# Two post-norm decoder layers on one core: an order of work written out stage by stage and tile by tile, with a PSUM bank for every fill

## The reference

```
x = norm(x + latent attention(x))          # l0: 16 heads, 32 latents, rotary tables, causal softmax
x = norm(x + linear attention(ctx, x))     # x0: q (k^T v), its own norm with gain and offset
x = norm(x + fp4 gated ffn(x))             # f0: 704 wide; x, weights and hidden are quantized in blocks of 16
x = norm(x + attention(x))                 # l1: causal softmax, and a second product over e = v - y
x = norm(x + cross attention(x, ctx, mask))# x1: softmax, Wo, norm, a 1024 wide relu ffn, norm
x = norm(x + fp6 linear(x))                # f1: x and weight quantized in blocks of 32
```

## Time and profile before

| | |
|---|---|
| time, median of 3 runs | 926.42 us (926.02 to 926.56) |
| time of the profiled execution | 925.68 us |
| its span, first to last instruction | 923.9 us |
| mean granted TensorE clock | 0.978 |
| TensorE busy | 827.3 us, 90% |
| VectorE busy | 712.0 us, 77% |
| ScalarE busy | 637.5 us, 69% |
| GpSimd busy | 300.6 us, 33% |

### The profile page before, as it was taken

The page is one execution under the profiler, slowest core; times in us unless marked ns, Lnnn a source line. Parts: engine busy times, 40 slices in busy tenths (PEclk is TensorE's granted clock), DMA queues, the critical chain, the costliest instruction groups (busy, mean ns, idle before and its releaser), DMA issues.

```text
span 923.9 us, 29437 instructions
## 1 busy us (share of the span) xinstructions
PE 827.3 (90%) x11910; PEld 661.0 (72%) x11910; DVE 712.0 (77%) x1619; ACT 637.5 (69%) x2507; POOL 300.6 (33%) x554
## 2 busy tenths in 40 slices
PE   4576789999999999999999999999999999988873
PEld 3454567777878787878788787878787877867642
DVE  6886586878797878878787978788787878786552
ACT  2434669595968688786959686877869686856541
POOL 1121222233243434243333434342433334242221
PEclk8888999999999999999999999999999999999997
DMA  9300200000100000000001000000000000000000
GB/s 327 142 6 10 94 9 22 2 25 2 36 2 27 12 17 17 13 19 8 28 2 33 9 25 11 22 16 7 20 8 28 11 7 11 11 7 6 9 1 12
DMA packets 24440, 24.87 MB, mean 27 GB/s; under 512 B 2304, under 2 KB 22640, under 8 KB 24176
## 3 DMA queue, kind: packets, MB, share of 16 engines
q1 hardware_dynamic: 24304, 22.98, 7.6%
HBM read 18.80 MB, written 2.10 MB: 23 GB/s over the span
## 4 chain that ended last, share of the span: by engine, by line
PE 67%; ACT 18%; DVE 8%; POOL 3%; issue 2%; DMA 1%; SPq 0%; DVEq 0%; POOLq 0%; ACTq 0%
PE bank L1284 39%; PE s_tile L1284 21%; ACT prob L771 9%; PE bank L1405 3%; PE bank L1495 2%; ACT k_ L804 2%; POOL rstd L638 1%; DVE rope_ L1051 1%; ACT probT L710 1%; ACT x_ L819 1%; DVE stats L1001 1%; DVE y_ L1014 1%; ACT cross_ L795 1%; PE bank L1525 1%; ACT xt_ L856 1%
## 5 line engine op out<-in xcount | busy, mean ns | idle before, releaser
L771 ACT ACTIVATE prob<-s_tile,low 128x128 f32<-128x128 f32 x768 | 273.2, 402 | 6.6 <-DVE low L1059 6.5
L771 ACT ACTIVATION_READ_ACCUMULATOR prob<-s_tile,low 128x1 f32 x768 | 186.0, 242 | 0.0
L1059 DVE TENSOR_REDUCE low<-s_tile 128x4 f32<-128x512 f32 x192 | 121.1, 680 | 19.8 <-PE s_tile L1284 19.8
L636 POOL TENSOR_TENSOR var_eps<-mean_var,rsq 128x1 f32<-128x1 f32 x144 | 31.3, 218 | 267.3 <-DVE mean_var L1003 267.3
L710 ACT ACTIVATE probT<-bank 128x512 f32<-128x512 f32 x192 | 99.7, 618 | 24.0 <-PE bank L1495 23.9
L638 POOL TENSOR_TENSOR rstd<-var_eps,rsq 128x1 f32<-128x1 f32 x144 | 87.2, 606 | 11.3
L710 ACT ACTIVATE xt_<-bank 128x256 f32<-128x256 f32 x64 | 24.6, 384 | 87.5 <-PE bank L1405 87.3
L1284 PE MATMUL bank<-w_gu,xt_ 128*128 128x352 f32 x256 | 78.4, 459 | 0.6 <-ACT xt_ L710 0.6
L1495 PE MATMUL bank<-cst,prob 32*128 32x32 f32 x3072 | 61.6, 225 | 19.0 <-ACT prob L771 12.8
L1495 PEld LDWEIGHTS bank<-cst,prob 32*128 32x128 f32 x3072 | 54.0, 138 | 32.5 <-ACT prob L771 15.0
L673 POOL TENSOR_TENSOR k_<-q_,q_scale 128x256 f32<-128x256 f32 x32 | 19.8, 620 | 176.2 <-DVE q_ L962 176.2
(11 more groups left out here) (200 smaller groups left out, 1948.9 us busy)
## 6 DMA issues: line engine op xcount, KB each, us to landing
xtin<-in_xT SPq DMA_DIRECT2D x16, 128.0 KB, 2.3
next_<-in_x SPq DMA_DIRECT2D x16, 128.0 KB, 6.8
ct_<-in_ctxT SPq DMA_DIRECT2D x16, 128.0 KB, 7.5
w<-in_w SPq DMA_DIRECT2D x2, 1024.0 KB, 6.7
out<-x_ SPq DMA_DIRECT2D x16, 128.0 KB, 1.9
next_<-x_ SPq DMA_DIRECT2D x16, 127.0 KB
rowt<-in_rows SPq DMA_DIRECT2D x1, 1664.0 KB, 9.0
w<-in_gate_up SPq DMA_DIRECT2D x2, 512.0 KB, 6.5
```

The source lines that it names most:

```text
L636: pool.tensor_tensor(var_eps[:, b:b + 1], mean_var[:, b, 1:2], rsq[:, 0:1], ALU.add) .then_inc(eps_in, 1)
L771: ins = act.activation(prob[:, r, c * P:(c + 1) * P], bank[r][:, c * P:(c + 1) * P], ACT.Exp, bias=low[:, b, at0:at0 + 1], accum_out=sums[ ...
L1059: dve.tensor_reduce(low[:, b, 4 * r:4 * r + 4], rows4(src[:, :]), AX_X, ALU.max, negate=True)\
```

## The change

The two tables `START` and `SLOTS` go. In their place stands `ORDER_AT`, which gives each stage of each engine a place in that engine's order for every tile, so that the distance between tiles can differ from stage to stage and from tile to tile. `BANKS` gets a digit for each tile and fill. `COVERED` is written anew for the new order. Since the order no longer keeps certain distances by itself, four waits are added. The stages, their instructions and their number are the same on the four compute engines; on SP the entries that did nothing are no longer listed.

On TensorE the first places are now the seven stages warm0, 12, 1, 5, 7, 3 and 2, then l0_project of tile 0; all 14 warm stages stand in the first 49 places.

```diff
-START = (0, 2381, 4750, 7129, 9503, 11883, 14256, 16632, 19008, 21379, 23760, 26136, 28512, 30885, 33264,
-         35642)
-SLOTS = dict(
-    PE=dict(v_bias=0, turn_up0=1340, cproj_bias=4139, warm1=6077, l0_project=6248, x0_kv=8380, l0_lat=8504,
...
+ORDER_AT = dict(
+    PE=dict(warm0=0, warm12=1, warm1=2, warm5=3, warm7=4, warm3=5, warm2=6, l0_project=(7, 11, 19, 25, 32, 225, 243, 278,
+        311, 448, 467, 505, 536, 672, 693, 731), v_bias=8, l0_lat=(9, 14, 24, 28, 222, 241, 277, 309, 446, 465, 502,
...
+        x1_scores=(146, 178, 209, 246, 370, 400, 434, 470, 594, 623, 657, 695, 812, 846, 876, 893),
...
+    DVE=dict(quant_up0=0, columns=1, round_up0=2, v_bias=3, l0_rope=(4, 6, 17, 19, 171, 185, 216, 245, 351, 365, 396, 425,
...
-BANKS = {"p_g": 5, "p_qk0": 5, "p_qk1": 4, "p_v": 6, "l0_project.qk": 7, "l0_v.v": 5, "l0_lat.s0": 0,
...
+    "l0_mix0.t0": '5475633532073676', "l0_mix0.t1": '3551361767550005', "l0_mix0.t2": '4244027406144747',
...
-    steps = [(START[t] + slot[stage], t, n, stage) for n, stage in enumerate(STAGES) if stage in slot
-             for t in range(TILES)]
...
+    steps = [(n, stage, t) for stage, places in ORDER_AT[engine].items()
+             for t, n in enumerate(places if isinstance(places, tuple) else (places,))]
+    return [(stage, t) for _, stage, t in sorted(steps)]
...
                 pool.wait_ge(came_x[b], came_by(i, 1, 1))
+                if i > 0:
+                    wait_empty(pool, i - 1, ("f1_out", b, "o"))
                 pool.tensor_tensor(xb_[:, b, :], next_[:, b, :], cproj_bias, ALU.add).then_inc(x_biased, 1)
...
+                    if stage == "l0_out" and i > 0:
+                        normed(dve, i - 1, "f1_norm", b)
                     emptied(dve.tensor_tensor(y_[:, b, :], src[:, 0:D], other[:, b, :], ALU.add), i, key)
...
+                    if n == 2 and i + b > 0:
+                        dve.wait_ge(k_done, i * GROUP + b)
...
+                if i * GROUP + b >= 2:
+                    wait_full(dve, i, ("x1_scores", b - 2, "s3"))
```

More of the change, by code:

```diff
@@ L67 @@
 PIECES = ("up0", "up1", "up2", "down0", "down1", "last")
-START = (0, 2381, 4750, 7129, 9503, 11883, 14256, 16632, 19008, 21379, 23760, 26136, 28512, 30885, 33264,
-         35642)
-SLOTS = dict(
-    PE=dict(v_bias=0, turn_up0=1340, cproj_bias=4139, warm1=6077, l0_project=6248, x0_kv=8380, l0_lat=8504,
[L74 to L108, removed]
-)
@@ L190, in plan_banks @@
     used, where = [0] * 8, {}
-    fills = [(name, name) for name in SETUP_FILLS]
+    fills = [(name, BANKS[name]) for name in SETUP_FILLS]
     for stage, t in ORDER["PE"]:
-        fills += [(name, name) if stage in SETUP_STAGES else ((stage, t, name), stage + "." + name)
+        fills += [(name, BANKS[name]) if stage in SETUP_STAGES else ((stage, t, name), int(BANKS[stage + "." + name][t]))
                   for name in STAGE_FILLS.get(stage, [])]
-    for key, fill in fills:
-        k = BANKS[fill]
+    for key, k in fills:
         where[key] = (k, used[k])
@@ new lines @@
+    ("l0_mix0", "free.t3"): 0xf16a, ("l0_mix0", "l0_scores.s2"): 0xaddd, ("l0_mix1", "l0_scores.s3"): 0xbfff,
+    ("l0_mix2", "l0_scores.s0"): 0xfdd9, ("l0_mix3", "l0_scores.s1"): 0xccc9, ("l0_out", "free.o"): 0xad4e,
+    ("l0_out", "l0_value.y"): 0x2040, ("l0_project", "came_xT"): 0xeee0, ("l0_project", "free.qk"): 0xb9e8,
+    ("l0_scores", "free.s0"): 0x7cdb, ("l0_scores", "free.s1"): 0xffff, ("l0_scores", "free.s2"): 0xf7d5,
+    ("l0_scores", "free.s3"): 0xdd37, ("l0_scores", "k_done"): 0xaaaf, ("l0_scores", "l0_lat.s3"): 0x5550,
@@ new lines @@
+    ("l1_mix2", "l1_scores.s0"): 0x7fef, ("l1_mix3", "l1_scores.s1"): 0x46af, ("l1_out", "free.o"): 0xf156,
+    ("l1_out", "l1_ma_value.y"): 0x2110, ("l1_project", "free.k"): 0xc913, ("l1_project", "free.qk2"): 0xabd3,
+    ("l1_project", "l1_turn_x.xt"): 0x01a2, ("l1_scores", "free.s0"): 0xc7fa, ("l1_scores", "free.s1"): 0xb97d,
+    ("l1_scores", "free.s2"): 0xfdd7, ("l1_scores", "free.s3"): 0x373b, ("l1_scores", "l0_lat.s3"): 0x1000,
+    ("l1_scores", "l1_project.k"): 0x778f, ("l1_scores", "l1q_done"): 0xfffc, ("l1_spread", "free.iv"): 0x064c,
@@ L481, in run @@
         def run(engine, table):
-            assert set(table) == set(SLOTS[engine])
+            assert set(table) == set(ORDER_AT[engine])
             for stage, t in ORDER[engine]:
```

225 lines of the change are left out of this document (183 added, 42 removed), and 44 rows, old and new, of the table BANKS.

## The result

The kernel after takes 916.12 us (median of 4 runs, 914.32 to 917.54) against 926.36 us for the kernel before beside it (4 runs, 926.02 to 926.56): a ratio of 0.989 with a 95% interval of 0.987 to 0.991. It is faster, by 10 us where 39 were forecast, and 2 us above the range. All ratios here are to the kernel before, run alongside. The profiled execution has a span of 913.9 us.

The account below looks back on a forecast made before the run. TensorE, busy 827.3 of 923.9 us, was taken as the bound: 838 us to x1_scores of tile 15, 43.4 to the end and 4 for the clock make 885 us of span, with 1.8 around it 887 us; range 862 to 914.

Parts of the forecast that it names:

- Filling: Pipeline's start, to x1_scores of tile 0: four tiles' l0_project brought forward cut TensorE's lag from 59 to 23 us, gain 36.
- x1_scores 8.8 us later as now: Tile 0: x1_scores follows l1_out's residual on VectorE (147 us) by 8.8 us as before, so at 156 us.
- lag: TensorE's time at a row less the work ordered ahead of it; forecast 23 us at x1_scores of tile 0.
- Setup and warm stages: Seven warm stages ahead of l0_project of tile 0: nothing; none left in the tail: 4 us lost to a lower clock.
- The period: Full pipeline: waits of 2.8 us a tile, with seams 3.8 where it was 2.7; 50 us of lag over 13.2 tiles.
- seams: Time between TensorE's stages in the full pipeline beyond work and waits, about 1.05 us a tile.
- nothing, bound 4 us: SBUF collisions of VectorE and GpSimd: removing them gains nothing, at most 4 us.
- Draining: Pipeline's end: x1_scores of tile 15 at 838 us, then 43.4 us to the end as before.
- The period gets worse by more than filling gives: Rival, full pipeline: in-order waits take 6.8 us of lag a tile or more; 936 us at 7.5; chance 0.12.
- The head does not fill: Rival, pipeline's start: VectorE's lag stays 38 us and TensorE's 41; 905 us; chance 0.13.
- The change does only what its name says: Rival, whole kernel: collisions go, filling and period come out even; 3.7 us, 922 us; chance 0.04.
- The clock falls in the tail: Rival, from x1_scores of tile 15 on: TensorE at half its clock without warm stages, some 20 us, 903 us; chance 0.06.

Follow-up runs that it names:

- e5: Kernel before with only its eleven late warm stages moved to where the kernel after has them; 937.06 us, ratio 1.011.
- e3: Kernel after with ten more warm stages in waits of the middle and seven more in the tail; 904.98 us, ratio 0.975.
- e1: Kernel after with ten more warm stages inside waits ahead of the clock's six falls between 245 and 494 us; 907.10 us, ratio 0.978.
- e10: Kernel after with half of the exponentials left out; 904.52 us, ratio 0.976.
- e12: e3 with GpSimd's 112 passes into xb_ cut from 256 columns to one; 898.62 us, ratio 0.969.
- e4: Kernel before with six waits ahead of l1_mix made longer by moving x0_kv and f1_turn_x of six tiles each behind it; 952.99 us, ratio 1.027.

## Why the prediction was wrong

**Filling: right in kind, 7.5 us short.** The steps to l1_out came true (VectorE at 148.5 against 147, busy 94% where over 85% was named). The step that failed is "x1_scores 8.8 us later as now". In the old order 8.6 us of TensorE's work stand between the two; in the new one 19 stages with 15.5 us do, and the measured distance on TensorE is 16.2 us. The distance was copied from the old rows although the list of the new order was at hand. The lag won at x1_scores of tile 0 is 28 us, not 36. How much of the 28 is order and how much a head at the full clock was not told apart (e5).

**Setup and warm stages.** "Nothing" for the seven in front was counted with their time in the work ahead, and f0_up of tile 0 at 90.5 us bears it out. e5 prices all eleven moved ones, in the old order, at a loss of some 10 us; what they cost in the new one was not measured apart, except that seven put back into the tail (with ten in the middle, e3) bring 3 us there.

**The period: the largest error, 21 us of 28.9.** Two steps failed, and both are in TensorE's busy time. The first is the clock, which was priced in "Warm stages" for the tail alone (4 us, measured 3) and as a rival "in the tail", while 10 us were lost in the full pipeline (e1, e3). The prediction said itself that some waits would be 2 to 4 us long where they had been 0.8, and added them up as if only their sum counted. Behind some of the waits TensorE ran at half its clock for some microseconds, 30.7 us in all, though it idled no longer than the 34.3 us between the same two stages before. The Trainium skill ("TensorE: Matmul & The Clock Gate", section "A second HAM failure mode: psum-queue depth-cycling") says that frequent short idle gaps between groups of matmuls make the clock go up and down. The trace agrees for four of the six falls, which stand behind gaps of at most 0.81 us. It doesn't for the kernel before, whose gaps of 0.65 and 0.8 us in every tile, 9 us apart, left the clock at 1.00 between 500 and 600 us.

The second is the term for seams, "about 1.05 us", carried over from nine tiles of the old order. In e3, with only 3.4 us left at 1.2 GHz in the period, TensorE is busy for 658.3 us without the ten warm stages, 26.3 more than the 632 us of work: 2.0 us a tile. That is 12 us over the 14 of the sum. What they consist of is open: seams, stages that run slower in the new neighbourhood, or work priced too low from the old rows.

The waits, which the prediction named as the whole of the loss, came out at 33.4 us, under its 37. That was luck in part, for they are not where it had them. It had 2.5 of its 2.8 us a tile before the mix stages of three softmaxes; measured, the waits that end on exponentials are 7.1 us in the whole period, and e10, with half of the exponentials, idles as long. The long ones it did not foresee: "Banks per fill move no work" is true, but the four longest waits are each for a bank that another stage's reader had not yet emptied. xb_ passes one column wide take another 3 us of waits out of the period (e12), for which the prediction had "nothing, bound 4 us".

**Draining: right**, 47.3 us against 47.4, and its 4 us for the clock are about right too: e3, with the tail's clock up, takes 44.5.

**The rivals.** "The period gets worse by more than filling gives" named the right place and the wrong mechanism: 5.4 us a tile, where 6.8 would have decided, and none of what went beyond the forecast was waiting. "The head does not fill" is wrong: 28 us of lag were won. "The change does only what its name says" is wrong as well: the COPY's mean does fall, from 408 to 339 ns, but the new order makes other collisions, 8.2 us of removable VectorE time against 1.2. "The clock falls in the tail" named the right resource at the wrong place. The range's own bounds held term by term (head lag 13 to 41, measured 30.5; period 2.0 to 5.5, measured 5.4); that two of them would be used at once was left out, and the result lies 2 us above.

**What stays open.** What the 12 us of busy time beyond clock and forecast seams consist of. Why the clock falls behind some waits and not behind others of the same length. What the banks cost as a whole could not be tried apart from the order: with one order and the other's banks the engines would wait for each other in a ring. The four added waits were not tried alone either, since the order needs them. With e12 as the measure the head lacks 9 us as well (164.9 us to x1_scores of tile 0, forecast 156), and its tail of 42.4 us is 1 shorter than the 43.4 that stood in the sum ahead of the clock's 4.

## What to carry to other kernels

When an order of work is changed, compare not only the sum of the bottleneck engine's waits but how they lie: 34 us of them, spread evenly over the old order, left the clock alone in the profiled run; 33 us in single long waits and in short ones close together went with 30.7 us at half clock, and ten throw-away matmul stages inside them won 10 us back. Compare the engine's busy time too: the same matmuls in another order were busy for longer. Count the work that stands between two points in the new order, instead of carrying a distance over from the old trace. And before you speed up what an engine waits for, look at what is due next: half of the exponentials left out was worth 5 us of 926.

## What the runs showed of the hardware

- A TensorE that was 94 to 96% busy over 100 us still had its clock at 1.2 GHz for 6 to 10% of the time (means of 0.95 to 0.97). The falls stood behind single waits of 2.39 and 1.96 us, one of 0.81 us, and groups of two or three of 0.3 to 1.1 us within 4 us; behind others as long (2.64 us) there was none. Which waits do it is not fixed: the same kernel had mean clocks of 0.961 to 0.981 and times of 923.6 to 912.2 us.
- From run to run of one kernel a microsecond more at 1.2 GHz went with about a third of a microsecond more of time, not the half by which TensorE falls behind in it. Why the rest is won back was not tested; in e4 the busy time grew by the full half (15 us for 30.7).
- A 0.485 us pass of VectorE with two SBUF inputs took 1.38 us beside a GpSimd pass of 1.45 us, and five of 32 such passes were slow in one order and none in the other. A one-input pass of 0.41 us took up to 0.81.
- Leaving out half of the exponentials, 125 us of ScalarE's time, left TensorE idle for as long (34.2 us against 33.4): other waits, of the same total, ended last.
